# Per-batch scatter waits, a third row of last products, one-by-one lead rows, a moved fill and moved divisions

## The reference, cut to what matters

```python
x = x + 0.5 * ffn(layernorm(x), gate_w, Wg, Wu, Wd, Ws_g, Ws_u, Ws_d)
x = x + attn(layernorm(x), Wq, bq, Wk, bk, Wv, bv, Wo, bo)
x = x + 0.5 * ffn(layernorm(x), gate_w, Wg, Wu, Wd, Ws_g, Ws_u, Ws_d)

def ffn(h):                                   # 16 experts, 512 hidden columns
    scores = softmax(h @ gate_w.T).transpose(0, 2, 1)
    topk_w, topk_idx = top_k(scores, 256)     # each expert takes 256 tokens of each batch
    g, u = x_tok @ Wg[e].T, x_tok @ Wu[e].T
    eo = ((gelu(g) * u) @ Wd[e].T) * topk_w
    flat = zeros.at[flat_idx].add(eo)         # added to the tokens' rows
    return flat + (gelu(h @ Ws_g.T) * (h @ Ws_u.T)) @ Ws_d.T
```

## Time and profile before

| | |
|---|---|
| median of 3 runs | 1594.68 us (1594.64 to 1594.71) |
| the profiled execution | 1593.02 us |
| its span, first to last instruction | 1591.3 us |
| mean granted TensorE clock | 0.987 of full |
| TensorE busy | 1516.4 us, 95% |
| ScalarE busy | 982.3 us, 62% |
| VectorE busy | 891.6 us, 56% |
| GpSimd busy | 552.5 us, 35% |

### The profile page before, as it was taken

The page is one execution under the profiler, slowest core; times in us unless marked ns, Lnnn a source line. Parts: engine busy times, 40 slices in busy tenths (PEclk is TensorE's granted clock), DMA queues, the critical chain, the costliest instruction groups (busy, mean ns, idle before and its releaser), DMA issues. The chain is left out here.

```text
span 1591.3 us, 26650 instructions
## 1 busy us (share of the span) xinstructions
PE 1516.4 (95%) x10009; PEld 1058.0 (66%) x10009; DVE 891.6 (56%) x1949; ACT 982.3 (62%) x1332; POOL 552.5 (35%) x494
## 2 busy tenths in 40 slices
PE   5899999999998979999999999999899999999997
PEld 4788888888986863333333333333688888888896
DVE  6787766666755961113144332132788857666673
ACT  7322254445434869999999999997632235444542
POOL 3000246566644971112111022120300035566644
PEclk9999999999999989999999999999899999999999
DMA  8231156666646699505235344020513136666653
GB/s 281 69 104 54 46 157 162 148 153 143 160 79 154 238 279 172 77 6 82 44 79 109 103 72 74 10 67 27 179 42 105 41 97 163 158 148 154 149 125 40
DMA packets 121377, 181.05 MB, mean 114 GB/s; under 512 B 19040, under 2 KB 83040, under 8 KB 118496
## 3 DMA queue, kind: packets, MB, share of 16 engines
q1 hardware_dynamic: 92784, 130.56, 31.3%
q0 software_dynamic: 28464, 48.78, 15.1%
HBM read 123.73 MB, written 55.57 MB: 113 GB/s over the span
## 5 line engine op out<-in xcount | busy, mean ns | idle before, releaser
L1989 ACT ACTIVATE 8215_pr<-8215_pS 128x1024 f32<-128x1024 f32 x448 | 421.8, 1081 | 12.6 <-PE 8215_pS L1910 11.4
L1940 PE MATMUL 8215_pO<-8215_pr,6314_vres 128*32 128x512 f32 x1792 | 239.3, 606 | 4.6 <-DVE 8215_tO L2014 3.3
L1910 PEld LDWEIGHTS 8215_pS<-sq_rows,sk_rows 50*128 50x128 f32 x896 | 74.7, 185 | 202.9 <-ACT 8215_pr L1989 159.4
L1910 PE MATMUL 8215_pS<-sq_rows,sk_rows 50*128 50x512 f32 x896 | 186.2, 467 | 10.1 <-PEq L1542 5.6
L2014 DVE STREAM_TRANSPOSE 8215_tO<-8215_pO 128x512 f32<-128x512 f32 (+1 forms) x33 | 23.0, 699 | 258.1 <-PE 8215_pO L1940 255.3
L190 PE MATMUL 15182_pGU<-columns_XT,weights_wts 128*128 128x512 f32 x384 | 152.6, 397 | 1.6 <-DVE columns_XT L947 1.6
L190 PE MATMUL 116_pGU<-columns_XT,weights_wts 128*128 128x512 f32 x384 | 152.6, 397 | 1.6 <-DVE columns_XT L947 1.6
L787 ACT ACTIVATE hidden_hT<-116_hf 128x512 fp32r<-128x512 f32 x96 | 60.7, 632 | 144.6 <-DVE 116_hf L937 144.6
L191 PE MATMUL 116_pGU<-columns_XT,weights_wts 128*128 128x512 f32 x384 | 149.7, 390 | 0.0
L191 PE MATMUL 15182_pGU<-columns_XT,weights_wts 128*128 128x512 f32 x384 | 149.7, 390 | 0.0
L192 PE MATMUL 15182_pGU<-columns_XT,weights_wts 128*128 128x512 f32 x384 | 149.7, 390 | 0.0
(11 more groups left out here) (387 smaller groups left out, 3438.6 us busy)
## 6 DMA issues: line engine op xcount, KB each, us to landing
116_raw_g<-WgT SPq DMA_DIRECT2D x16, 512.0 KB, 4.0
116_raw_u<-WuT SPq DMA_DIRECT2D x16, 512.0 KB, 3.5
116_raw_d<-WdT SPq DMA_DIRECT2D x16, 512.0 KB, 4.3
q_rows<-rows_halves SPq DMA_DIRECT2D x8, 1024.0 KB, 4.9
k_rows<-rows_halves SPq DMA_DIRECT2D x8, 1024.0 KB, 5.1
15182_raw_g<-WgT SPq DMA_DIRECT2D x16, 512.0 KB, 3.9
15182_raw_u<-WuT SPq DMA_DIRECT2D x16, 512.0 KB, 3.6
15182_raw_d<-WdT SPq DMA_DIRECT2D x16, 512.0 KB, 4.0
```

The lines of the kernel that those rows point to most:

```text
L1910: m = t_.matmul(to[:, e, :], key, query, start=True, stop=True)
L1940: m = t_.matmul(pO[e * 32:(e + 1) * 32, off:off + wd], vres[:, (g // GB) * TPB + kt, at:at + 32], from_(e), start=n == first[j], stop=n == ...
L1989: s_exp.done(a.activation(to, pS[:, u % RING, :, :], ACT.Exp, scale=HD ** -0.5))
```

## The change

It has five parts. **(a)** `s_sc` becomes four signals, one for each buffer and batch. A scatter of one batch waits for the scatters of the same batch alone; GpSimd waits twice per expert, ahead of q = 0 and of q = 2, and VectorE per half. The last expert's scatters count on the same signals as all. **(b)** `last_down` does chunks 0 to 2 of three results ahead of the wait for chunk 3, where it did those of two. **(c)** SP loads `lead_x1` only when `lead_x0` has landed. **(d)** The fill of `sk` comes behind the first `turned`, where it stood ahead of it. **(e)** Both divisions of the last block of heads come ahead of both splits.

```diff
-            s_sc = [sig(f"scattered{k}", 64) for k in range(2)]
+            s_sc = [[sig(f"scattered{k}{b}", 32) for b in range(B)] for k in range(2)]
...
                     s_wl.wait(sp, 3 * E)
-                    for k in range(2):
-                        s_so[k].wait(sp, J // 2 + 1)
+                    s_sc[1][0].wait(sp, E // 2)
                     for q in range(2):
                         self.counter(f"proj_x_lead{q}", 16).done(sp.dma_start(self.lead_x[q][:, :, :], ov[q]))
+                        if q == 0:
+                            self.counter("proj_x_lead0", 16).wait(sp, 1)
...
-                    for q in range(2):
+                    for q in range(3):
                         for c in range(FC - 1):
                             rows_down(d, q, c, own_bank(q))
                     t_.wait_ge(*s_hl.at(4 * (d + 1)))
                     for q in range(4):
-                        for c in range(FC - 1 if q < 2 else 0, FC):
+                        for c in range(FC - 1 if q < 3 else 0, FC):
                             m = rows_down(d, q, c, own_bank(q))
                         s_Dq.done(m)
...
                             s_so[k].wait(v, J // 2)
-                            s_sc[k].wait(v, (d - J) // 2)
                             s_wt.wait(v, d - J + 1)
+                    if d >= J:
+                        s_sc[k][h].wait(v, (d - J) // 2)
...
-                    else:
-                        s_sc[1 - k].wait(g, (e - 1) // 2 + 1)
                     rows_ = idx[:, e, :, :].rearrange("p b h -> p (b h)")
                     for q in range(4):
+                        if e > 0 and q % 2 == 0:
+                            s_sc[1 - k][q // 2].wait(g, (e - 1) // 2 + 1)
...
-                g.wait_ge(*s_xn.at(2))
-                s_clear.done(g.memset(self.sk[:, 0, :, :].bitcast(f32), 1.0))
...
                 for n in range(2 * J - 1):
                     turned(n)
+                    if n == 0:
+                        g.wait_ge(*s_xn.at(2))
+                        s_clear.done(g.memset(self.sk[:, 0, :, :].bitcast(f32), 1.0))
...
                 for again in range(2):
                     heads_of(j, slice(8 * again, 8 * again + 8), again)
+                for again in range(2):
                     split(*quads[-1], slice(256 * again, 256 * again + 256), again)
```

More of the change, by code:

```diff
@@ L572, in _ @@
                     s_wl.wait(sp, 3 * E)
-                    for k in range(2):
-                        s_so[k].wait(sp, J // 2 + 1)
+                    s_sc[1][0].wait(sp, E // 2)
                     for q in range(2):
                         self.counter(f"proj_x_lead{q}", 16).done(sp.dma_start(self.lead_x[q][:, :, :], ov[q]))
+                        if q == 0:
+                            self.counter("proj_x_lead0", 16).wait(sp, 1)
                 for k in range(2):
-                    s_sc[k].wait(sp, E // 2 - k / 2)
-                    s_so[k].wait(sp, J // 2 + 1)
+                    for b in range(B):
+                        s_sc[k][b].wait(sp, E // 2)
             @blk.tensor
@@ L970, in evacuate_last @@
                     k = d % 2
-                    s_sc[k].wait(v, (d - J) // 2)
                     s_wt.wait(v, d - J + 1)
                     for q in range(4):
+                        s_sc[k][q // 2].wait(v, (d - J) // 2)
                         v.wait_ge(*s_Dq.at(q + 1))
@@ L1130, in scatter @@
                             self.settle(g)
-                        sent = g.indirect_dma_start(out, bass.IndirectOffsetOnAxis(rows_[:, q:q + 1], 0), eo[:, k, q, :],
-                                                    None, compute_op=ALU.add)
-                        if item == NI - 1 and q < 2:
-                            s_so[q].done(sent)
-                        else:
-                            s_sc[k].part(sent, 16)
+                        s_sc[k][q // 2].part(g.indirect_dma_start(out, bass.IndirectOffsetOnAxis(rows_[:, q:q + 1], 0), eo[:, k, q, :],
+                                                                  None, compute_op=ALU.add), 16)
                 def split_shared(w):
```

2 lines of the change are left out of this document (1 added, 1 removed).

## The result

The change took 1598.19 us in the median of 15 runs (1596.23 to 1602.5), the kernel before 1594.68 (1593.05 to 1596.87, 15 runs on the same chip). The medians differ by 3.5 us; the ratio is 1.0023, with an interval of 1.0016 to 1.0030, which is 2.6 to 4.8 us slower. The forecast was 1596.1, with a range of 1593.4 to 1598.6. The time lies inside the range, near its slow edge, and 0.23% is just past the 0.2% that I had given 0.13.

The account below looks back on a forecast made before the run. The prediction took TensorE, busy 1516.4 of 1591.3 us, as the bound, with room only where it stands still. Tail +1.08, lead +1.0 and divisions -0.7 gave +1.4 on 1594.68: 1596.1 us, range 1593.4 to 1598.6.

Parts of the forecast that it names:

- (a): Scatter waits per batch, in the experts and the tail: the removed waits cost nothing, the added one is already satisfied; 0.
- (b): Last expert's third row: no second pause, nine more products ahead of result 0 delay the scatter chain; tail +1.08 us.
- (c): Lead loads one by one, at the first `ffn`'s end: second load lands at 500.05 against 499.11 needed; +1.0 us.
- (d): Fill of `sk` in `projections`: its 3.52 us fit GpSimd's 4.07 us wait between two `turned`, 0.55 us left; 0.
- (e): Divisions at attention's end: the second pair fits the 0.70 us wait, second transpose at some 1111.2; -0.7 us.
- The sign: Whole kernel: slower, by +1.4 us or 0.09%, no change that can be told.
- late second quad: Rival at the lead's first use: loads take 4.9 and 5.8 us, lead +3.2, time 1598.3 us; chance 0.13.
- Now: 487.66 + 3.86 = 491.52: First `ffn`'s end: second scatter starts 1.08 us later, and SP issues the lead loads 3.86 us after its start.
- estimate of 3.2 us: Lead loads by the skill's rule for 512 KB: seam 0.6 us earlier than before, sum below -0.2 us.
- The clock: Rival at the second `ffn`'s start: a 1.2 GHz stretch drops or is added, 1594.3 or 1597.9 us; chance 0.16.
- loads alone are quick: Rival at the lead: both loads take 3.8 us, the lead pays 0.1, time 1595.2 us; chance 0.22.

Follow-up runs that it names:

- e4: The change with VectorE's operation on `lead_w` moved ahead of the last expert's four scalings; 1598.33 us, ratio 1.0024 to the kernel before.
- e2: The change with both lead loads issued at once, without the wait between them; 1599.92 us, ratio 1.0030 to the kernel before.
- e5: The kernel before with three results' early products ahead of the wait for chunk 3 and nothing else changed; 1599.2 us, ratio 1.0022.
- e7: The change with 100 instead of 64 products on constants after the first layer's last expert; 1598.98 us, ratio 1.0022 to the kernel before.
- e9: The change with 128 instead of 64 products on constants after the first layer's last expert; 1600.01 us, ratio 1.0034 to the kernel before.
- e10: The change with two results ahead of the wait for chunk 3 and the lead loads issued together; 1594.92 us, ratio 1.0003 to the kernel before.
- e11: The kernel before with one result's early products ahead of the wait instead of two, nothing else changed; 1594.07 us, ratio 0.9994.
- e1: The change with two results ahead of the wait for chunk 3 in place of three; 1595.24 us, ratio 1.0007 to the kernel before.
- e3: The change with one result ahead of the wait for chunk 3 in place of three; 1592.98 us, ratio 0.9987 to the kernel before.

## Why the prediction was right, and where it was off

The sign was right and the size was not: +1.4 us forecast, +3.5 in the medians. Point by point:

- **(a) 0**: right where the prediction looked, since the tail's scatters keep their 0.30 us. It did not count on VectorE's added waits costing anything, and in every kernel with (a) 0.35 us more go by ahead of VectorE's last multiplication, for a reason that no row shows. **(d) 0**: borne out. The fill has 0.61 us of room (0.55 forecast).
- **(b) +1.08 in the tail**: +1.06, and 27 products without a pause. This was the part that a description ("in the pause") would have got wrong. The earlier trace rows decided it: VectorE's low half of chunk 3 was done 1.5 us before TensorE had worked through the rows that it had.
- **(e) -0.7**: -0.51, the near end of its range. The prediction put the second transpose at "some 1111.2", 1.31 us behind the first; it came 1.49 us behind. The other 0.15 us of the -0.66 in G are TensorE's clock.
- **(c) the lead, +1.0**: the size was off, and so was the path. Its loads came as sized or sooner (4.4 and 3.8 against 4.7 and 3.8) and the rival of a late second quad fell. The prediction put the whole +1.0 on the second load (500.05 against 499.11). In the trace that load has 0.15 us at the most, and the first load carries the delay. The step that failed is "Now: 487.66 + 3.86 = 491.52", where the second scatter was moved by 1.08 us with its length kept. It moved behind the start of VectorE's `lead_w` operation, which the third row does not delay (result 3 completes when it did), and it took 2.59 us. From the low halves to the first rotation the change pays 1.63 us in place of 1.0; with that scatter free (e4) it pays 0.74. The other kernels with three rows pay 1.9 to 2.1 there (e2, e5, e7, e9), since their C or D is longer. The prediction also set an estimate of 3.2 us against its own. The Trainium skill, "DMA: Bandwidth & Descriptors", section "Anatomy of one DMA", states its figures for transfers that GpSimd issues; SP issued these loads, and none landed in under 3.8 us.
- **The clock, left at 0 and kept as a rival** (0.16): with the scatter it was the largest miss in the profiled execution, E +1.02 and F +0.78. For E e9 and the order of the thirteen kernels show the cause. For F no run removed it. Where the low stretch ends 8.5 to 9.5 us after the fill, F is 513.65 to 513.90 (six kernels), and 514.25 to 514.59 where it ends 10.2 to 11.2 us after it (six); e9 stands outside, with 8.2 and 514.49. H is not the clock's: behind its start the change has 3.4 us at 1.2 GHz and the kernel before 9.8. Nor does E's miss belong to the third row alone: e10 and e11 have E at 87.52 and 87.60 with two rows and one. The runs have a mean granted clock of 0.985 for the change and 0.987 for the kernel before (the 32 runs beside e1 to e4); among those at 0.987 and above, the change averages 1596.67 us (three runs) and the kernel before 1594.06 (21), +2.6.

So the sum of the terms as measured is 1.10 + 0.53 (B and C) + 1.06 - 0.51 + 0.35 = +2.5, close to the +2.6 of the runs at a like clock. That the rest up to 3.5 is the clock fits, and is not shown. The rivals: "loads alone are quick" was right on the loads and wrong on the time. "The second quad late" named the time, 1598.3, by a mechanism that did not happen. The time lies inside the stated range only because that rival stretched it to 1598.6, and that was luck. The miss was a neighbour on another engine, 0.35 us on VectorE that come with (a), and the clock.

## What to carry to other kernels

Work moved "into a pause" is free only if the engine still pauses at that place: compare the end of what it waits for with the end of what it has in hand, and if the wait was already satisfied, put less ahead of the first result, not more, where a chain of later steps hangs on that result. When a step shifts against another engine, look at what it now starts under, and search the trace for a row of the same operation with an odd length. Gains below a microsecond are read between landmarks of the trace, since the total moves by more from one execution to the next (1596.23 to 1602.5 us for the change). Then look for the same difference in every kernel that has the edit and in none that lacks it.

## What the runs showed of the hardware

**A VectorE operation with two SBUF inputs holds a GpSimd scatter that starts under it.** The scatter took 1.55 us alone. Started while VectorE had 1.17 us of its 1.75 us operation left it took 2.59 (change), with 1.10 left 2.52 (e5), with 1.48 left 2.90 (e3), with 0.33 left 1.75 (before): the rest of the operation less some 0.13 us is added each time. A scatter that started first (486.58, with VectorE from 487.01) took 1.55. The same is in the experts of the kernel before, where 24 scatters started with 0.75 to 0.94 us of such an operation left and took 2.21 to 2.37 us. Another 24 started with 0.20 to 0.25 us left of a multiplication of which one input lies in PSUM, and took 1.55 to 1.57. One scatter of each `ffn` started with 0.4 us left of a scaling out of PSUM, and took 1.62. One of the 24, GpSimd and then VectorE:

```profile
441.04 2.28 POOL L1131 DMA_INDIRECT x_after_ffn<-116_eo,116_idx  x1 [0.30 <-issue]
```

```profile
440.65 1.23 DVE L527 TENSOR_TENSOR weights_wts<-116_raw_d,weights_wts 128x1024 fp32r<-128x1024 f32 x1
```

The Trainium skill, "SBUF — State Buffer", section "Who interferes with whom", says that a VectorE instruction with two SBUF inputs contends with a GpSimd instruction that reads SBUF, with which these rows agree. It also infers that `tensor_tensor` does not hold back the writing of descriptors for a GpSimd DMA. Here the whole instruction was held (2.59 and 2.90 us); since an indirect scatter reads its row numbers too, no run here shows which part of it waited.

**A load of 512 KB** landed after 3.8 us at the best, alone; the first lead load, with the second held back and the last scatters beside it, took 3.9 us (e3) to 4.8 (e9).

**TensorE's granted clock** fell to 0.50 in the tail of some executions: in e2 and e4 18 products ran at 1.2 GHz there, and the first result came 1.5 us later, though neither differs from the change at that place. Four kernels with three rows did not show it.
